# Issuing the expert-weight loads before the barrier, and moving the gate stores from the SyncE queue to the GpSimd queue

## The reference

```python
xn = _layernorm(x, axis=-1)
s  = _L0_attn_ref(xn, qw, kw, vw, ow)     # 16 heads of 64, rope, causal softmax
g  = _silu(_L0_ffn_ref(xn, Wg, We, be))
return x + s * g

# _L0_ffn_ref: 8 experts, the best two weighted by a softmax of their gate logits
vals, sel = jax.lax.top_k(xt @ Wg.T, 2)
w = jax.nn.softmax(vals, axis=1)
y = einsum('td,eod->teo', xt, We) + be    # every expert for every token
out = einsum('tk,tko->to', w, take(y, sel))
```

## Time and profile before

| | us |
|---|---|
| median of 2 runs | 2865.4 (2859.3 to 2871.5) |
| the profiled execution | 2859.8 |
| its span on the slowest core (core 1), first to last instruction | 2858.3 |
| spans of the 8 cores | 2843.5 to 2858.3 |
| busy on core 1: PE / DVE / ACT / POOL | 2180.6 / 992.0 / 962.4 / 461.8 |

### The profile page before, as it was taken

The page is one execution under the profiler, slowest core; times in us unless marked ns, Lnnn a source line. Parts: engine busy times, 40 slices in busy tenths (PEclk is TensorE's granted clock), DMA queues, the critical chain, the costliest instruction groups (busy, mean ns, idle before and its releaser), DMA issues.

```text
span 2858.3 us, 30318 instructions; the slowest of 8 cores (2843.5 to 2858.3 us)
## 1 busy us (share of the span) xinstructions
PE 2180.6 (76%) x9976; PEld 817.8 (29%) x9976; DVE 992.0 (35%) x1529; ACT 962.4 (34%) x1373; POOL 461.8 (16%) x543
## 2 busy tenths in 40 slices
PE   1888888469977995999599807777788347677787
PEld 0333333424433442444244301121211101121211
DVE  3576676424432441344144303221201213221212
ACT  2444442110010002000200004647587134657574
POOL 0466666200000000000000002211111021211110
PEclk9999999569988997999799955888888757788888
DMA  4299932074416524550743080210010532020100
GB/s 130 75 163 174 166 109 82 24 118 60 60 47 101 79 40 89 84 93 1 142 65 59 19 215 4 74 56 19 25 35 1 136 72 74 1 74 1 59 1 30
DMA packets 382533, 203.94 MB, mean 71 GB/s; under 512 B 342944, under 2 KB 351136, under 8 KB 381872
## 3 DMA queue, kind: packets, MB, share of 16 engines
q1 hardware_dynamic: 370160, 142.76, 24.9%
q0 software_dynamic: 12224, 59.27, 9.8%
HBM read 84.28 MB, written 67.37 MB: 53 GB/s over the span
## 4 chain that ended last, share of the span: by engine, by line
PE 61%; ACT 12%; SPq 8%; issue 7%; POOL 5%; DVE 4%; DMA 2%; ACTq 0%; POOLq 0%; DVEq 0%
PE PA L673 16%; PE PB L673 15%; ACT AR L857 8%; SPq L237 7%; PE PV L776 6%; POOL AR L868 5%; PE PA L902 4%; PE PA L419 4%; PE PB L419 4%; PE PC L419 4%; PE PA L847 2%; PE PB L847 2%; ACT AR L786 2%; PE PV L359 1%; PE PC L545 1%
## 5 line engine op out<-in xcount | busy, mean ns | idle before, releaser
L673 PE MATMUL PA<-AR 128*128 128x512 f16 x2048 | 471.8, 384 | 27.1 <-DMA AR<-we 27.1
L776 PE MATMUL PV<-AR 128*128 128x512 f16 (+6 forms) x1280 | 419.3, 418 | 66.9 <-POOL AR L868 66.8
L673 PE MATMUL PB<-AR 128*128 128x512 f16 x2048 | 462.9, 379 | 0.0
L857 ACT ACTIVATE AR<-PA 128x1024 f16<-128x1024 f32 x320 | 302.7, 946 | 249.1 <-PE PA L847 246.7
L847 PE MATMUL PA<-AR 64*128 64x512 f16 x640 | 149.9, 460 | 292.0 <-ACT AR L857 142.0
L683 DVE SCALAR_TENSOR_TENSOR AR<-PA,wm,AR 128x512 f32<-128x512 f32 x256 | 192.2, 751 | 420.5 <-PE PA L673 226.2
L857 ACT ACTIVATE AR<-PB 128x1024 f16<-128x1024 f32 (+1 forms) x320 | 275.8, 862 | 92.1 <-PE PB L847 92.0
L868 POOL TENSOR_TENSOR AR<-AR,tri 128x256 f16<-128x256 f16 x256 | 170.7, 667 | 819.4 <-ACT AR L857 795.5
L673 PEld LDWEIGHTS PA<-AR 128*128 128x128 f16 x2048 | 202.4, 99 | 276.3 <-issue 40.5
L683 DVE SCALAR_TENSOR_TENSOR AR<-PB,wm,AR 128x512 f32<-128x512 f32 x256 | 192.2, 751 | 250.2 <-PE PB L673 232.1
L818 DVE TENSOR_TENSOR AR<-AR,PC 64x512 f16<-64x512 f32 x64 | 43.5, 679 | 664.1 <-PE PC L812 662.9
(11 more groups left out here) (99 smaller groups left out, 1689.4 us busy)
## 6 DMA issues: line engine op xcount, KB each, us to landing
we<-we POOLq DMA_DIRECT2D x8, 2048.0 KB, 24.8
out_c<-AR SPq DMA_DIRECT2D x8, 2048.0 KB, 8.9
v_sp<-AR POOLq DMA_DIRECT2D x32, 264.0 KB, 3.5
AR<-v_sp POOLq DMA_DIRECT2D x2, 4224.0 KB, 26.0
AR<-x_c SPq DMA_DIRECT2D x32, 256.0 KB, 10.8
k_sp<-AR POOLq DMA_DIRECT2D x32, 256.0 KB, 4.4
q_sp<-AR SPq DMA_DIRECT2D x32, 256.0 KB, 4.5
g_sp<-AR SPq DMA_DIRECT2D x32, 256.0 KB, 2.0
```

Source lines behind the costliest of these rows:

```text
L673: sl=slots[ib], half=half: e.matmul(PG[:, 512 * ib:512 * ib + 512], lhs, sl[:, c * D + half * 512: c * D + (half + 1) * 512], start=(c == ...
L776: nkc=nkc, p2=p2, mw=mw: e.matmul(PV2[0:mw, 512 * p2 + w0:512 * p2 + 512], v_sb[:, kc * VF + h * VW:kc * VF + h * VW + mw], expb3[sbk][:, ...
L857: W("scalar", lambda e, PS=PS, sbk=sbk, ev=ev: e.activation(ev(expb3[sbk]), ev(PS), AF.Exp, scale=1.0 / 32.0), waits=[("eT", C["eT"]), ("e ...
```

## The change

Two edits. The first alters the waits of the expert-weight loads: not the last barrier, but the counts that PE, DVE and POOL had at the end of the loop of stage 1, and the four semaphores of the cosine tables. The second moves the store of g from SP's queue to POOL's.

```diff
@@ -538,6 +538,8 @@
             if 6 <= it < NT + 6:
                 p1a(it - 6)
 
+        loopT, loopV, loopP = C["eT"], C["eV"], C["eP"]
+
         for t in range(NT):
@@ -643,8 +645,10 @@
-                ldw = P.bw() + [("swe", wew), ("eT", slot_free.get(sp, 0)),
-                                ("scsA", C["scsA"]), ("scsB", C["scsB"])]
+                ldw = [("eT", max(slot_free.get(sp, 0), loopT)),
+                       ("eV", loopV), ("eP", loopP), ("swe", wew),
+                       ("scsA", C["scsA"]), ("scsB", C["scsB"]),
+                       ("scsC", C["scsC"]), ("scsD", C["scsD"])]
                 for (sl, ee) in ((slots[0], e0), (slots[1], e1)):
@@ -698,7 +702,7 @@
-                dma("sync", g_sp[gt * 128:(gt + 1) * 128, :], g_st[p][:, :],
+                dma("gpsimd", g_sp[gt * 128:(gt + 1) * 128, :], g_st[p][:, :],
                     sg_, waits=[("eA", C["eA"])])
```

## The result

The changed kernel is slower: 2887.35 us (median of 12 runs) against 2865.79 us (11 runs of the kernel before on the same chip), a ratio of 1.0086 with a 95% interval of 1.0067 to 1.0106, thus about 25 us. This is within the 2% that were named as the limit of what a measurement can tell, but its interval is clear of 1, it is outside the range given, and on the other side of no change than forecast. (In some executions a few cores show a lower granted clock and take longer; the ratios leave out those that are much longer by it, medians don't, and mean spans are compared only between the rows "before", "after", "second edit only" and "pair 1 held back", whose profiles are free of it.)

The account below looks back on a forecast made before the run. The prediction took PE's gaps before the four quarters of stage 3 and that stage's end as the bound; - 23.8 us gained, + 1.4 and + 13.1 for slower stores gave -9.3 against 2859.8, thus 2850 us, range 2838 to 2874.

Parts of the forecast that it names:

- What bounds the gaps: Between quarters of stage 3, Silus then bias turns or weight transposes delay PE's restart; transposes end last, by some seven us.
- The gain: Four gaps before the quarters of stage 3: PE's wait for weights shrinks from 27.1 us, 23.8 us gained.
- The step for the first edit: Before quarter 0: weight loads no longer wait for the barrier, gaining 6.0 of 6.83 us of PE idle.
- its cover: Before quarter 0: pair 0's weights are in place at 553, PE could use them from 603, so 50 us spare.
- The pacing of the Silu phase: In each gap, two Silus then a wait for a store's landing: 3.25 us a pair, three waits per gap.
- The size of L in the gaps: Issue to landing of a store of g from POOL before quarters 1 to 3: 3.5 us, costing 13.1 us.
- the collision: In the gaps before quarters 1 to 3, 16 transposes of pair 1 run 25 us over the 15 us Silu phase.
- Its count of packets: In the gaps, a store of g is 128 rows of 2 KB, 8 packets on each of 16 engines.
- The second rival: In the gaps, stores stand behind the transposes: landing of 4.5 us or more, 2860 to 2882 us; chance 0.30.
- The end of stage 3: Before attention: four steps, each 0.36 us longer with stores landing in 2.4 us from POOL, costing 1.4 us.
- The sum: Whole kernel: - 23.8 + 1.4 + 13.1 = -9.3 us, giving 2850 us.
- The third rival: On SP's queue: something unseen holds it, so loads don't come earlier and only cost is left, 2874 us; chance 0.05.

Follow-up runs that it names:

- second edit only: The kernel before with only the stores of g moved to POOL's queue, weight loads still waiting for the barrier; ratio 1.0129 to the kernel before.
- pair 1 held back: Changed kernel, but in quarters 1 to 3 pair 1's transposes wait for the last Silu of the quarter before; ratio 0.9998 to the kernel before.
- The run with one transpose at a time: Changed kernel, pair 1's transposes in the gaps before quarters 1 to 3 each wait until the one before landed; no ratio, mean span 2857.7 us.
- the plain loads: Changed kernel with pair 1's transposes in quarters 1 to 3 replaced by plain loads of the same bytes; no ratio, mean span 2893.8 us.
- run 25: No run of this name or number occurs in the text given, so no change or time can be stated.

## Why the prediction was wrong

By its own steps:

- **What bounds the gaps: right.** Two paths from PE's last matmul to its restart, a common Silu phase, and the bias turns as the one that is left. After the change PE waits 0.82 us for the last bias copy in all four gaps, to the hundredth what the step said.
- **The gain: right.** 18.7 us over the mean of the cores. The 23.8 us were worked out for core 1, whose four bias phases of before add up to 115.1 us, against 110.0 in the mean; to 91.3 after, that is 23.8 for core 1 and 18.7 for the mean. The step for the first edit (6.0 us on core 1) is right too, and its cover held.
- **The pacing of the Silu phase: right in form.** Three steps in a gap, each the longer by what the landing grows, and by POOL's later issue, which the step left out.
- **The size of L in the gaps: wrong, and the step that failed.** The prediction saw the collision, gave its ends as 2.4 and 7.0, and took 3.5, "nearer to the lower end since the packets in the way are small". Measured: the stores land in 4.8 to 5.2 us (medians of the three gaps over the cores), and a Silu waits for the slower of the two stores before it, which takes 5.6 us in the mean. A step grew by 35.9 / 9 = 4.0 us instead of 1.46: 3.6 from 2.04 to 5.6, and some 0.4 because POOL issues later than SP. That is an effective L of 6.0; with the quiet price of 0.75 taken off, 3.2 us of company. The run with one transpose at a time shows the mistake: there the packets are as small and the store loses only 0.8 us in a step (2.4 / 3), and beside the plain loads, whose packets are some seven times as large (1.8 KB in the mean), the Silu phases are within 1.4 us of those beside the full stream. The size of the packets was the wrong thing to go by. What counts is what the other queue has in flight, and the prediction had that, three transposes with a landing of 4.6 us, and weighed it lower. Its count of packets was off too, without weight: from POOL's queue a store is 64 packets of 4 KB, 4 on each engine, and not 8 (page of before against page of after, see below). The cost of the gaps was 35.9 us, not 13.1.
- **The second rival was what happened**, as far as runs show it: L is above 4.5, which turns the sign, and within its bounds (a landing of 5.0 at the median, an effective 6.0, of at most 7.0). That the stores stand only behind the transposes ahead of them is not shown, by the last stores of "pair 1 held back". With the end of stage 3 the loss in the phases is 24.3 us, even more than the +22 given as its bound, since the mean of the cores has 5 us less to gain than core 1. The chance of 0.30 was too small, and the range ended at 2874 where the rival's own bound was 2882.
- **The end of stage 3: wrong in size, 7.1 us instead of 1.4.** The four steps of 0.36 were taken from the landing alone. POOL's issue comes 0.48 us after its semaphore, which made each step 0.75, and the barrier now waits for POOL's drain. That "nothing else waits behind them there but the barrier" was said and not priced.
- **The sum.** From -9.3 to +24.3 us in the phases are 33.6: 22.8 from the gaps, 5.7 from the end of stage 3, and 5.1 because the mean of the cores had less to gain than core 1.
- **The third rival did not happen**: on core 4 the transposes run from 518.9 us on and again from 767.4, 168 us after PE's restart as the prediction had it, and in the gaps from PE's last matmul on.

The slices above have packets of both queues in the same microsecond. The Trainium skill's rule that an engine takes turns between its queues (DMA: Bandwidth & Descriptors, "Queues, rings and completion order") is compatible with that, but the trace does not show it engine by engine, and the small loss that the prediction drew from it did not come. The landings by gap (medians of 5.6, 4.6 and 5.0 us, core 4) are near the transposes' own 4.6. The same section of the Trainium skill has the rule that a completion waits for the engine's earlier writes, of other queues too. That would show as time between the store's last packet and its landing, which grew only from 0.4 to between 0.7 and 1.0 us, while more was lost before and between its packets. So the rule can account for the smaller part of the delay at most; why the packets themselves come late stays open.

## What to carry to other kernels

Moving a transfer to another queue frees what stood behind it, and what is freed goes at once: ask which burst will now run beside the moved transfer, and whether anything waits for it to land. A small store beside a stream of loads lands about when the load issued just ahead of it lands, here mostly 4 to 8 us instead of 2, from POOL's queue as from ACT's; either let nothing wait for it (more buffers), or keep the order of one queue and put only the load that is needed ahead of it. Price a landing beside other traffic by the landing of that traffic, not by the bytes of the store.

## What the runs showed of the hardware

- A store of 256 KB to DRAM lands in 2.0 us from SP or ACT and 2.3 from POOL when alone, in 4.7 to 5.2 us (medians of the gaps over the cores) beside a stream of transposes, from POOL as from ACT, and in 2.5 to 2.9 when the transposes go one at a time. Behind plain loads in flight on SP's queue it took up to 8.8 us.
- The same store is 144 packets from SP or ACT and 80 from POOL. On the pages of before and after, POOL's queue goes from 12224 packets to 14784 for 32 stores and SP's from 370160 to 365552; without the 16 tiny ones of each store these are 128 of 2 KB and 64 of 4 KB.
- POOL issues a transfer 0.48 us after the semaphore that it waits for has come (changed kernel, first gap). SP needs 0.03 (kernel before, same place).
- A drain on POOL ended 3.7 us after the issue of the last store ahead of it. Before, with no store in POOL's queue, POOL issued its first load of attention at 1646.89, 0.8 us after ACT's last Silu. Whether the drain waits for the transfer itself or for something else in POOL wasn't told apart.
- ACT and PE in turns on one PSUM tile take 1.43 us (22.9 / 16) for a bias matmul and its copy of 0.58 and 0.59 us; on two tiles 0.75 us (12.1 / 16).
